# Last layer of a graph network: the running base per lane and tile kept by VectorE in SBUF instead of by 25 identity products per block on TensorE

## The reference, cut to what matters

```
h   = max(layernorm(x), 0)
msg = h[dst] * edge_weight[:, None]             # edge_index = (src, dst): row = src, col = dst
agg = segment_sum(msg, src, num_segments=12500)
x   = x + h @ W_self.T + b_self + agg @ W_neigh.T + b_neigh
```

## Time and profile before

| | us |
|---|---|
| median of 3 runs | 16642.69 |
| lowest and highest run | 16616.44, 16654.34 |
| profiled execution, first to last instruction (the only time that its page gives) | 16655.4 |
| last layer's loop over blocks, from the first scatter to the last | 11226.9 to 15889.6 |

### The profile page before, as it was taken

The page is one execution under the profiler, slowest core; times in us unless marked ns, Lnnn a source line. Parts: engine busy times, 40 slices in busy tenths (PEclk is TensorE's granted clock), DMA queues, the critical chain, the costliest instruction groups (busy, mean ns, idle before and its releaser), DMA issues. The chain is left out here.

```text
span 16655.4 us, 228031 instructions
## 1 busy us (share of the span) xinstructions
PE 7442.4 (45%) x71916; PEld 5270.8 (32%) x71916; DVE 8010.3 (48%) x11391; ACT 6068.0 (36%) x10705; POOL 7332.9 (44%) x7085
## 2 busy tenths in 40 slices
PE   1244444454444544446988999960000000000055
PEld 1133333343333433333544555530000000000045
DVE  4255555555555555555444434444444444444475
ACT  0132323333333333335777777742222222222200
POOL 4444444444444544433111111136666666666610
PEclk9855555655655555568999989965555555555587
DMA  6333333333333333335655656632222222222186
GB/s 265 131 97 109 98 109 97 110 107 99 109 97 110 110 97 110 98 102 147 203 174 175 204 155 204 204 112 57 58 56 55 57 58 56 57 55 58 48 290 225
DMA packets 1622965, 1983.45 MB, mean 119 GB/s; under 512 B 513957, under 2 KB 1419270, under 8 KB 1617497
## 3 DMA queue, kind: packets, MB, share of 16 engines
q1 hardware_dynamic: 1302057, 1257.39, 25.7%
q10 hardware_dynamic: 94032, 435.46, 6.4%
q0 software_dynamic: 226176, 281.93, 6.1%
HBM read 1171.70 MB, written 816.17 MB: 119 GB/s over the span
## 5 line engine op out<-in xcount | busy, mean ns | idle before, releaser
L645 POOL DMA_INDIRECT RF<-tab_edge_b,idx x3125 | 3236.0, 1036 | 3666.1 <-DMA idx<-e_src 2659.8
L1208 POOL DMA_INDIRECT records<-RF,idx x3125 | 3092.0, 989 | 1597.5 <-issue 990.9
L698 DVE TENSOR_TENSOR HM<-iota_b,eqw 128x2048 bf16<-128x2048 bf16 x2000 | 2192.1, 1097 | 2833.1 <-remote 1632.3
L1969 PE MATMUL bk<-HM 128*128 128x98 bf16 x16000 | 1637.7, 257 | 3164.9 <-issue 1606.4
L1809 ACT ACTIVATE X<-bk 128x392 uint8<-128x392 f32 x4000 | 1808.6, 495 | 2479.3 <-remote 1340.3
L1969 PEld LDWEIGHTS bk<-HM 128*128 128x128 bf16 x16000 | 1152.0, 120 | 3647.1 <-issue 3558.5
L1969 PE MATMUL kp<-HM,ident_b 128*128 128x98 bf16 x3125 | 275.2, 282 | 4380.6 <-DVEq L1718 2422.7
L782 PE MATMUL tp<-HM,RF 128*64 128x512 bf16 x12276 | 2003.6, 379 | 6.1 <-DVE HM L743 1.1
L882 POOL DMA_INDIRECT agg<-RF,lastT x372 | 528.3, 1420 | 2864.9 <-ACT RF L821 2774.1
L1969 PEld LDWEIGHTS kp<-HM,ident_b 128*128 128x128 bf16 x3125 | 251.6, 142 | 4405.1 <-issue 4405.1
L788 PE MATMUL om<-HM,RF 128*64 128x512 bf16 x6138 | 1451.4, 379 | 0.0
(11 more groups left out here) (376 smaller groups left out, 14562.8 us busy)
## 6 DMA issues: line engine op xcount, KB each, us to landing
dst_f<-counts SPq DMA_DIRECT2D x465, 512.0 KB
RF<-first_rows SPq DMA_DIRECT2D x250, 800.0 KB
counts<-X ACTq DMA_DIRECT2D x250, 784.0 KB
RF<-records SPq DMA_DIRECT2D x220, 784.0 KB, 5.2
records<-pivots SPq DMA_DIRECT2D x120, 1400.0 KB
crow<-counts SPq DMA_DIRECT2D x279, 512.0 KB
first_rows<-RF ACTq DMA_DIRECT2D x25, 4000.0 KB
edge_rows<-RF ACTq DMA_DIRECT2D x125, 800.0 KB
```

The costliest lines, as they stand in the source:

```text
L645: e.indirect_dma_start(out=ring[:, r, j, :], out_offset=None, in_=table[:, :], in_offset=bass.IndirectOffsetOnAxis(ap=idx[:, r, own(j):own ...
L698: return e.tensor_tensor(to[:, 0:n, :].rearrange("p k (q h) -> p k q h", h=2), iota_b[:, 0:m].rearrange("p (q h) -> p q h", h=2).unsqueeze ...
L1208: e.indirect_dma_start(out=records[:, :], out_offset=bass.IndirectOffsetOnAxis(ap=idx2[:, r, j:j + 1], axis=0), in_=msgs[MSG_OF[r]][:, j, ...
L1969: return e.matmul(to, by_q, by_r, start=start, stop=stop, skip_group_check=True)
```

## The change

Ahead of the loop VectorE copies the base from PSUM to SBUF (into a table that is free by then). In each block it multiplies the one-hot with this copy instead of with PSUM, sums over tiles as before, then sums the same one-hot over the 25 edges (a reduction whose innermost step is 98 elements), and adds the 98 counts to the running base. TensorE's loop (the last part of the diff), and both semaphores between it and VectorE, are gone.

```diff
+            running_base, in_block = stat["rstd"][:, :], stat["tmp"][:, :]
+            chain(e.tensor_copy(running_base, base))
 
             def body4(i):
                 ...
-                    wait(e, "based", b)
-                    gate(e)
                     loop_chain(row_onehots(e, oh_lane, rtwice[:, :, :], TILES))
-                    loop_chain(e.tensor_tensor(at, oh_lane, base.unsqueeze(1).broadcast_to([P, K, TILES]), ALU.mult))
-                    e.sem_inc(sem("looked"), 1)
-                    loop_chain(e.tensor_reduce(out=atbase[:, :], in_=at, op=ALU.add, axis=AX.X))
+                    loop_chain(e.tensor_tensor(at, oh_lane, running_base.unsqueeze(1).broadcast_to([P, K, TILES]), ALU.mult))
+                    e.tensor_reduce(out=atbase[:, :], in_=at, op=ALU.add, axis=AX.X)
+                    loop_chain(e.tensor_reduce(out=in_block, in_=oh_lane.rearrange("p k q -> p q k"), op=ALU.add, axis=AX.X))
+                    loop_chain(e.tensor_tensor(running_base, running_base, in_block, ALU.add))
                     wait(e, f"moved{r}", i * (16 * K) + 16 * ITERS * K)
                     ...
-            e.wait_ge(sem("based"), BLOCKS)
             e.sem_inc(sem("cleared"), 1)
 ...
-            def body4(i):
-                for r in range(R):
-                    wait(e, "looked", i * R + (r + 1))
-                    gate(e)
-                    for j in range(K):
-                        last = whole(base, ident_b[:, :], oh_lane[:, j, :], False, j == K - 1)
-                    last.then_inc(sem("based"), 1)
-            loop(e, body4)
```

## The result

The changed kernel takes 16328.67 us (median of 4 runs, 16298.59 to 16357.98) against 16632.49 before: ratio 0.9823, interval 0.9802 to 0.9843, 304 us faster. I had forecast 16530, 114 us less than the 16642.69 of before, with 16460 to 16610 as the range of that case. The direction and the place are as forecast, the size is not.

What follows compares the result with a forecast made beforehand. POOL's scatters were taken as the path, with idle time for late `targets`; 36.46 us per block against 37.39 saves 114 us over 123 blocks, 16655.4 to 16541 by span, 16530 as median, range 16460 to 16610.

Steps and rivals of the forecast that it cites:

- What bounds the kernel; the wait for `based`: Last loop: the path goes through POOL's scatters; its 606.6 us idle for `targets` come from late inputs, often TensorE's `based`.
- late state: In the loop, after POOL scatters without rest, engines' posts become visible late, the later the more instructions they just issued.
- ScalarE takes over most of what `based` gives up: Last loop: ScalarE's chain becomes the late one, leaving a gain of 0.93 us per block, 114 us over 123 blocks.
- my rounds: Loop blocks between POOL's rests: one round of three blocks to three of four, 36.46 us per block against 37.39.
- Hold on a scatter, 1.5 us per block, 33.7 in all: L1717 with two SBUF tables delays POOL's scatter 1.5 us per block; the 25 scatters then cost 33.7 us.
- The reduction at 2.71 us: VectorE's new sum over 25 edges takes 2.71 us per block, bounds 1.44 and 4.0.
- But then POOL has had no rest and the state stays late.: Last loop: a round without POOL's rest stays late, so its fourth block is ready about 144.5 us; four blocks take 145.4.
- Rival A: Late posting eases too, as TensorE's 50 instructions per block stop posting: 16200, or 16280 with some rests left; chance 0.15.
- B: Last loop: nothing is gained, ScalarE's chain takes all: 16640; chance 0.12.
- C: Last loop: POOL's shorter rest shrinks the quick stretch, 115 us slower: 16760; chance 0.13.
- D: L698 waits for the port held by POOL's scatters, not for TensorE, and keeps waiting: +123 us, 16765; chance 0.05.

Runs made afterwards that it cites:

- e8: The kernel before, unchanged, run again for its profile in the second set: 16990.3 us, ratio 1.
- e3: The changed kernel with the running base left in PSUM, so L1717 holds no scatter: ratio 0.9777 to the kernel before.
- e7: The changed kernel, unchanged, run again for its profile in the second set: ratio 0.9740 to the kernel before.
- e1: The changed kernel with TensorE's 25 products per block put back, into a bank nobody reads: ratio 0.9819 to the kernel before.
- e2: The changed kernel with 5 TensorE products per block put back, into a bank nobody reads: ratio 0.9762 to the kernel before.
- e4: The kernel before with the base copied to SBUF for L1717, and `looked` posted before the product; TensorE's products stay: ratio 0.9757.
- e18: The changed kernel, unchanged, in the last set, where the kernel before takes 13473.4 us: ratio 1.0145.
- e15: The changed kernel with base in PSUM, ScalarE's activations as four VectorE products, their weights and L698's number row in PSUM: ratio 0.9825 to the kernel before.

## Why the prediction was wrong

- *What bounds the kernel; the wait for `based`.* Right. GpSimd is on the path, and with `based` gone its waits for `targets` fall from 787 to 300 us even with the late state kept (e8, e3).
- *"ScalarE takes over most of what `based` gives up".* Too much even with the state kept. By my rounds without a hold (36.34 - 32.2 = 4.1 us per block, about 510 us) 80% of GpSimd's 636 us of idle time would have stayed. In e3 53% did (429 of 806 us in e8), in the changed kernel 24% (152 of 636).
- *Hold on a scatter, 1.5 us per block, 33.7 in all.* Right: 2.44 us for the scatter beside L1717, 1.60 us per block, and 196 us for the whole kernel in the set without the late state. L1717 itself waited for no scatter: 2.71 us as before, with 4.3 us of idle time in front of all 124.
- *The reduction at 2.71 us.* Wrong, 4.39, outside my bounds. I see no cost of it in the time: VectorE waits 1.4 ms in the loop for ScalarE's planes. My row for a strided read was one copy of 25 elements, too short to show a cost per element. The rule in the Trainium skill that I quoted (page "Advanced Engine Details and Errata", section "Memory Cachelines") had the direction right; by my estimate from it, it would have been 5.3.
- *"But then POOL has had no rest and the state stays late."* This step failed. I had taken the state as a function of the last rest, from blocks 49 and 50: late from some 38 us of scattering on. In the changed kernel eight blocks in a row, some 290 us, are quick without such a rest. The term of the sum that it spoils is GpSimd's idle time in the rounds: 2.8 us per block (36.46 - 33.7), and 1.2 measured (152 us). ScalarE's waits fall from 212 to 64.
- *How much of the miss that is.* From the first scatter of block 0 to that of block 123 a block takes 35.2 us, where I had 36.46: 160 us of the 190 that the forecast lacks of the 304. Some 26 are the saving behind the loop, which I had left out. Set by set, and so only roughly: without a hold my rounds give 36.3 us (I had the hold at 15 us in all), and e3, late state and no hold, takes 35.8. So the rounds were too dear by about 65 us even with the state kept. With the hold e7 takes 35.4: in place of costing 15 us it gains about 45, another 60. The last 35 us or so lie between two profiles of the same kernel, e7 and the first.
- *Rival A* gave 16280 for its milder form, near the 16329 measured, for a wrong reason. That is luck. Taking TensorE's postings away leaves the state as it was (e3); where the hold is there they add to what is left of it (e1, e2). Rivals B, C and D did not occur: L698 waits for nothing, and the first block after a rest is quick.

The Trainium skill, "NOTIFIC — the notification-queue block", section "Interfaces", lists backpressure towards the producers of records when an internal FIFO fills, and says that this can stall an engine. A delay that grows with the instructions issued would look like this; no run here shows whether it is that, or whether the state would exist without a trace being taken.

## What to carry to other kernels

When semaphores arrive late while one engine issues scatters back to back, ask first what slows that engine: a hold that looks like pure cost (1.6 us per block) gave back more than it took in the sets that have the state (e3 against e7, e8 against e4), and was the whole loss in the one that has not. So one should look for the state in one's own profile before counting on it; a delay of 8 to 10 us behind eight short activations is its mark. The version with ScalarE's 25 small activations as four products of VectorE beats the changed kernel with the state (0.968 against 0.974, in two sets) and without it (1.010 against 1.015); without it the kernel before stays ahead of both.

## What the runs showed of the hardware that was not expected

- The same kernel took 16.6 ms, 17.0 ms and 13.5 ms in different sets, and two of these sets, 17.0 and 13.5 ms, have the same chip number. The fastest reached the last loop 2.7 ms earlier (8687 us in e18 against 11386 in e7), mostly by what GpSimd no longer waits for its indices in the first phase (3.5 us against 2820.7).
- Late hand-overs come in a fixed rhythm of blocks: two of three (82 of 125) in the kernel before, two of ten (24 of 125) in the changed one and in e4, three of ten in e7 (35 of 125).
- Five writes of 0.25 us, each waited for and one behind every fifth scatter (some 4 us per block in all), ended the late state; five in one place (2.7 us) or two in two places (1.6 us) did not.
- A product or compare of VectorE with two SBUF tables held the scatter that started beside it until 0.84 us after its own end; the same operation with one table in PSUM did not (scatters of 0.98 us on average in e15), at 2.71 us in place of 1.43 for L698.
- A reduction over 25 elements at a step of 196 bytes took 4.39 us for 2450 elements (bf16), and 2.71 with neighbours side by side (f32).
